# Transposes in place of identity products in three places of a four-layer graph network kernel

## The reference

```python
x = _layernorm(x + L0(x))   # two hypergraph convolutions, PReLU
x = _layernorm(x + L1(x))   # attention on leaky_relu(sent[s] + recv[r])
x = _layernorm(x + L2(x))   # attention, then out @ Wp + bp
x = _layernorm(x + L3(x))   # attention, ReLU, rows to unit length
```

```python
sent_proj = einsum('nd,dhk->nhk', nodes, W_s) + b_s
recv_proj = einsum('nd,dhk->nhk', nodes, W_r) + b_r
msg, r = sent_proj[senders], recv_proj[receivers]
logits = einsum('ehk,k->eh', leaky_relu(msg + r), a_w) + a_b
e = exp(logits - seg_max[receivers]);  w = e / denom[receivers]
agg = segment_sum(w * msg, receivers)
```

## Time and profile before

| | value |
|---|---|
| median of three executions | 5627.22 us |
| the profiled execution | 5618.88 us, of which the span is 5616.8 us |
| TensorE busy | 4348.7 us, 77% of the span |
| VectorE busy | 3708.2 us, 66% |
| ScalarE busy | 3066.9 us, 55% |
| GpSimd busy | 3225.3 us, 57% |
| mean granted TensorE clock | 0.858 of full |

### The profile page before, as it was taken

How to read it: one execution, slowest core, us unless ns; L and a number is a source line. 1 busy time by engine, 2 the same in 40 slices (tenths; PEclk the granted TensorE clock), 3 DMA queues, 4 the chain that set the end, 5 groups by cost and what they waited for, 6 DMA issues and landing times. The chain is left out here.

```text
span 5616.8 us, 80182 instructions
## 1 busy us (share of the span) xinstructions
PE 4348.7 (77%) x20170; PEld 3260.2 (58%) x20170; DVE 3708.2 (66%) x10668; ACT 3066.9 (55%) x8955; POOL 3225.3 (57%) x2882
## 2 busy tenths in 40 slices
PE   0344339899999799989688888869999997777675
PEld 0111116567777477777566777657878874554453
DVE  8522213445777476666478778757778778888886
ACT  0133225555899656555355555535555556766666
POOL 2577777762676545455356456534444347777774
PEclk9655559999999899999899889869999997877777
DMA  1478644443666556556445555535544434444441
GB/s 40 152 256 260 221 130 154 146 151 108 193 206 199 195 177 210 179 198 210 150 147 186 166 177 184 172 108 161 165 147 160 147 122 133 131 133 135 143 136 61
DMA packets 360222, 905.84 MB, mean 161 GB/s; under 512 B 69943, under 2 KB 144159, under 8 KB 359770
## 3 DMA queue, kind: packets, MB, share of 16 engines
q1 hardware_dynamic: 249578, 626.47, 32.9%
q0 software_dynamic: 110192, 274.25, 16.3%
HBM read 565.74 MB, written 340.13 MB: 161 GB/s over the span
## 5 line engine op out<-in xcount | busy, mean ns | idle before, releaser
L1067 PE MATMUL psum<-got,sf 128*128 128x256 f32 x1600 | 628.4, 481 | 441.5 <-ACT got L1325 399.8
L2320 POOL DMA_INDIRECT got<-tab,end_i x600 | 703.6, 1173 | 458.2 <-PE psum L1176 285.8
L2320 POOL DMA_INDIRECT got<-hop,end_i x600 | 643.7, 1073 | 434.7 <-PE psum L1067 201.6
L1067 PEld LDWEIGHTS psum<-got,sf 128*128 128x128 f32 x1600 | 322.8, 227 | 723.1 <-DMA got<-in_x,src_i 288.5
L1176 PE MATMUL psum<-got,sf 128*128 128x264 f32 (+2 forms) x1200 | 412.5, 430 | 250.3 <-DVE got L2045 201.0
L1971 DVE TENSOR_TENSOR res<-psum,own 128x512 f32<-128x512 f32 x300 | 206.3, 688 | 449.1 <-DMA own<-in_x,own_i 240.6
L1325 ACT COPY got<-psum 1x256 f32<-1x256 f32 x796 | 282.1, 354 | 401.0 <-PE psum L1067 274.0
L1176 PEld LDWEIGHTS psum<-got,sf 128*128 128x128 f32 x1200 | 225.5, 220 | 355.4 <-DVE got L2045 263.0
L1311 ACT CAST sf<-s 128x512 f32<-128x512 uint8 x350 | 214.4, 613 | 347.7 <-DVE s L1960 215.2
L1363 ACT ACTIVATE res<-res,l_mo 128x256 f32<-128x256 f32 x600 | 310.9, 589 | 140.7 <-DVE l_mo L1934 140.5
L1215 ACT ACTIVATE squares<-res,l_sv 128x256 f32<-128x256 f32 x600 | 297.3, 497 | 165.2 <-DVE l_sv L1946 106.8
(11 more groups left out here) (511 smaller groups left out, 12855.7 us busy)
## 6 DMA issues: line engine op xcount, KB each, us to landing
own<-hop SPq DMA_DIRECT2D x150, 512.0 KB
x_t<-res SPq DMA_DIRECT2D x150, 512.0 KB
xo<-x_t SPq DMA_DIRECT2D x150, 512.0 KB
hop<-res SPq DMA_DIRECT2D x100, 512.0 KB
tab<-tab SPq DMA_DIRECT2D x50, 536.0 KB
own<-tab SPq DMA_DIRECT2D x50, 536.0 KB
r_t<-rec_b SPq DMA_DIRECT2D x50, 528.0 KB, 3.7
rec_b<-r_t SPq DMA_DIRECT2D x50, 528.0 KB, 4.1
```

Source lines behind the costliest of these rows:

```text
L1067: T.matmul(o, sf_of(q)[:, k * P:(k + 1) * P], got_of(q)[:, k * FEAT:(k + 1) * FEAT], start=(p < 3), stop=True).then_inc(at("l_agg"), 1)
L2320: eng.indirect_dma_start(out=dst, out_offset=None, in_=table, in_offset=bass.IndirectOffsetOnAxis(ap=idx, axis=0), bounds_check=rows_ - 1, ...
```

## The change

Three products with the identity become transposes (`is_transpose=True`), and the planned lengths of these parts are set lower.

```diff
-                    put(("T", f"wp{h}", q), 1.73, here("Stz"), bank="ring", emptied=here(f"Vwp{h}"))
+                    put(("T", f"wp{h}", q), 1.3, here("Stz"), bank="ring", emptied=here(f"Vwp{h}"))
...
-                    put(("T", f"tab{k}", q), {3: 2.59, 4: 0.93, 5: 0.9}[p], here("Stp0", "Stp1"), bank="ring", emptied=here(f"{te}tab{k}"))
+                    put(("T", f"tab{k}", q), {3: 2.16, 4: 0.93, 5: 0.9}[p], here("Stp0", "Stp1"), bank="ring", emptied=here(f"{te}tab{k}"))
...
-                        put(("T", f"zq{c}", q), 1.8, here("Sselm", "Yrec", "Ggather"), bank="ring", emptied=here(f"Szq{c}"))
+                        put(("T", f"zq{c}", q), 1.4, here("Sselm", "Yrec", "Ggather"), bank="ring", emptied=here(f"Szq{c}"))
...
+        bs_m = sb("bs_m", [P, 2])
+        bc_m = sb("bc_m", [P, 2])
...
+                T.transpose(bank(6)[:, m * P:(m + 1) * P], bs[:, m * P:(m + 1) * P], ident[:])
+                T.transpose(bank(6)[:, (2 + m) * P:(3 + m) * P], bc[:, m * P:(m + 1) * P], ident[:])
...
                 if bias is not None:
-                    T.matmul(here, ident[:], bias[:], start=True, stop=False)
+                    for c in range(2):
+                        T.matmul(here[:, c * P:(c + 1) * P], bias[:, c:c + 1].to_broadcast([P, P]), ident[:], is_transpose=True, start=(c == 0), stop=False)
...
-                    half_product(eng, name, q, h, rows_t, ws, bias=bs)
+                    half_product(eng, name, q, h, rows_t, ws, bias=bs_m)
...
-                    T.matmul(o[:, k * P:(k + 1) * P], rows_[:, k, h * P:(h + 1) * P], sm[:, par, k * P:(k + 1) * P], start=True, stop=False)
-                    m = T.matmul(o[:, k * P:(k + 1) * P], sent[:, k, h * P:(h + 1) * P], ident[:], start=False, stop=True)
+                    T.matmul(o[:, k * P:(k + 1) * P], sent[:, k, h * P:(h + 1) * P], ident[:], is_transpose=True, start=True, stop=False)
+                    m = T.matmul(o[:, k * P:(k + 1) * P], rows_[:, k, h * P:(h + 1) * P], sm[:, par, k * P:(k + 1) * P], start=False, stop=True)
...
-                    T.matmul(here, ident[:], bc[:], start=True, stop=False)
+                    for c in range(2):
+                        T.matmul(here[:, c * P:(c + 1) * P], bc_m[:, c:c + 1].to_broadcast([P, P]), ident[:], is_transpose=True, start=(c == 0), stop=False)
...
+            V.tensor_copy(bs_m[:], bank(6).rearrange("p (c m) -> p c m", m=P)[:, 0:2, 0])
+            V.tensor_copy(bc_m[:], bank(6).rearrange("p (c m) -> p c m", m=P)[:, 2:4, 0])
```

## The result

The changed kernel takes 5643.16 us (median of 7 runs, 5636.19 to 5647.25) against 5627.22 us for the kernel before. The ratio is 1.0035, 95% interval 1.0023 to 1.0047: slower by 0.35%, where 1.7% faster was forecast. The profiled execution took 5643.6 us. One execution in this document is set aside, one of `h1` at 7718.2 us and a granted clock of 0.55, where the others of that kernel have 0.86.

A forecast was written before the change was run, and what follows sets the result against it. TensorE was taken to bound stage 5 outright and stage 3 nearly, sharing stage 4 with VectorE. From 5618.9 us, - 39 - 32 - 23 + 1 gave 5526, or 5534 as a median; range 5505 to 5565 (0.57).

The forecast's parts named there:

- the changed order: Stages 3 and 4: reordering of the engine lists, costed at nothing, with 15 us either way allowed in the range.
- Unit costs: TensorE, stages 3 to 5: 0.110 us per transpose against 0.223 per identity product and 0.43 per bias product, no stalls.
- Rival D: Stages 3 to 5: repeated-column transposes or adding onto a transpose cost more than before, 5638 us; 0.15 together with Rival C.
- Stage 5, -39 us: Stage 5: bias transposes in `wp` save 42 us of TensorE, of which 0.93 shortens the run, 39 us.
- Stage 3, -32 us: Stage 3: bias transposes in `tab` save 42 us of TensorE, of which 0.75 shortens the run, 32 us.
- the longer wait for the normalised rows: Stage 3: TensorE's 38.4 us wait for ScalarE's rows would grow, by as much as half the saving at the lower bound.
- Stage 4, -23 us: Stage 4: `zq` transposes save 45 us of TensorE, half counted because its waits interleave with VectorE's, 23 us.
- the alarm for the clock: Stage 4: a granted clock under 0.85 in the profile after would prove the forecast wrong.
- Preparation, +1 us: Before the stages: four more transposes and two small copies, all counted on the path, 1 us more.
- stage 6, 0: Stage 6: nothing there is edited, so its work and length stay the same, 0 us.
- Rival C: Stages 3 to 5: granted clock falls from 0.95 to 0.85 on average, giving 5642 us; 0.15 together with Rival D.
- Rival A: Only stage 5 pays, 39 us, since waits in stages 3 and 4 grow by the saving; 5589 us, chance 0.16.

The follow-up runs named there:

- h1: The kernel before, with its identity products, in the list order of g3; 5587.01 us, ratio 0.9940 to the kernel before.
- e1: The changed kernel with all its new operations, but the planned lengths and so the order of before; 5565.22 us, ratio 0.9893 to the kernel before.
- e2: The kernel before, with its products, but the planned lengths and so the order of the changed kernel; 5721.28 us, ratio 1.0179.
- g3: The changed kernel with `zq` and `wp` planned as before, `tab` at 2.23 and VectorE's stage 3 sum at 2.5; 5530.12 us, ratio 0.9829.
- f2: The changed kernel's operations planned with `tab` 2.7, `zq` 1.75, `wp` 1.73 and carry 0.45, which bunches the hops; 5661.41 us, ratio 1.0071.
- g1: The changed kernel's operations with planned lengths of before and a 2.5 us scheduler penalty on neighbouring hops or sums; 5729.95 us, ratio 1.0187.

## Why the prediction was wrong

The step that failed is the sentence on the changed order: "I cost both at nothing, and allow 15 us either way in the range, since a new list can meet the gathers elsewhere." The new list costs about 78 us with the new operations (5643 against 5565) and 100 us with the old. The prediction looked at a moved hop, found that the copy waiting for `tab` would be late by 0.87 us, and did not ask what the hop itself now stood behind: another hop, whose carry ScalarE had not copied, since its own list had other work first. In stage 3 this wait rose from 13.9 to 56.6 us. Nor did it ask what a sum moved earlier or a `zq` moved earlier in stage 4 would find ready; there TensorE came to wait 20.6 us for rows still on their way. The lengths in the change are not wrong (two chunks of a bias at 0.43 less 0.22 are 0.42 us, and 0.43 were taken off `tab`); the planner only has no price for an order that leaves no slack.

The other steps:

- Unit costs: right. Spacing 0.110 us for each kind of transpose, no price for changing between modes, and nothing to pay for the repeated column or for adding onto a transpose. Rival D is refuted.
- Stage 5, -39 us: mis-sized. In the old list it gave 27. Busy time fell by 33 us, not 42 (granted 0.94 instead of 0.95), and 6 us came back as idle time.
- Stage 3, -32 us: near, 26. Busy time fell by 40 us, and 14 us came back, mostly the longer wait for the normalised rows that was named.
- Stage 4, -23 us: mis-sized, 6. Busy time fell by 19 us instead of 45 and idle rose by 13. The lower clock accounts for the first in size: 789 less 45 is 744, and 744 x 0.88 / 0.85 is 770, which is what `e1` has. The longer idle time is TensorE waiting for VectorE's carry, 62.3 us against 39.5. The forecast of 0.85 as the alarm for the clock was just reached in `e1`, and the changed kernel passed it with 0.81.
- Preparation, +1 us, and stage 6, 0: nothing that could be told apart from them. Stage 3 begins 4 us later in the changed kernel, but runs with the same work ahead of it begin it anywhere from 1921 to 1933 us.
- Rival C gave 5642, within 2 us of what was measured, but by another path. It had the three stages fall to 0.85 because of the operations; with the operations in the old order they are granted 0.95, 0.85 and 0.94. So a part of it is real, in stage 4, where some 25 us of the busy time come back by it. The rival's number was also met by luck: from 0.95 to 0.85 busy time stretches by 12%, not 10, and with that its sum would have been some 5661. In stage 4 the old products in the new order are granted 0.84, and both edits together 0.81, so there each lowers the clock. In stage 3 neither does by itself (0.95 in `e1` and in `e2`), and only both together have 0.92; why, no run shows. The rule that full clock does not engage for transposes (the Trainium skill, "TensorE: Matmul & The Clock Gate", Part 4: PE-mode transpose) is not borne out in stage 3 of `e1`, which has 400 transposes in place of 200 products and is granted 0.95 as before. For stage 4 it is neither shown nor refuted, since there the transposes came and TensorE's busy share fell together. The earlier trace rows do not decide it either: products stand on both sides of the eight transposes, and at 3230.14 us, where a sum follows them, the clock had not risen yet.
- Rival A (only stage 5 pays, since waits grow in stages 3 and 4) describes stage 4 of `e1`, not the changed kernel.

With the order of before the time was 5565, the edge of the forecast's own range: the gains were put 31 us too high, and the order, put at nothing, cost 78.

## What to carry to other kernels

Where a list scheduler fixes the order, a change of its lengths is a change of the whole program: plan the new operations with the old lengths first, and judge a new order as an edit by itself. In an engine that runs its list in order, look at what each part now stands right behind: two links of a chain that passes through another engine should not be neighbours unless that engine answers at once, so its list has to be read too; and a gather should not be wanted soon after its buffer comes free. Lengths that describe the chip truly need not give the best list; a few lists tried on the chip were worth more here (`g3`) than half of the edit itself.

## What the runs showed of the hardware

- A transpose whose stationary operand is one column read 128 times runs at the spacing of one with a full block, 0.110 us, and a float32 product that adds to what a transpose wrote starts behind it with no gap.
- A carry through another engine is expensive where nothing covers it: 1.48 us from hop to neighbouring hop in the median against 0.87, and 3 us and more where the copy stands behind other work of ScalarE.
- With the new operations the granted clock of stage 3 is lower where the hops stall more: 0.95 in `e1`, 0.92 in the changed kernel, 0.89 in `f2` (TensorE busy 87%, 86% and 85% of the stage). With the old ones it is not: `e2` has the changed kernel's list, is busy 86%, and has 0.95. What lowers it is open.
- Sums side by side cost nothing in stage 6, where VectorE is busier than TensorE: against `e1`, `g1` took their number from 53 to 9 and the stall from 163 to 17 us, and stage 6 with the tail kept its 1053 us (1051).
